# Queries and keys in parts: from float32 transposes to FR matmuls with a unit matrix, in a kernel of four transformer layers on one core

## The reference

```python
x = x + L0_xattn(ln(x), ctx)          # 16 heads of 8, cross attention
x = x + L0_ffn(ln(x))                 # norm, 8 experts of 512, gelu
x = x + L1_xattn(ln(x), ctx)          # 32 heads of 4, padding and key masks
x = x + L1_ffn(ln(x))                 # top 2 of 8 experts, with a capacity
x = x + L2_xattn(ln(x), ctx)          # 16 heads of 8, scores + slope * (i - j)
x = x + L2_ffn(ln(x))                 # int8 matmul with scales
x = x + L3_xattn(ln(x), ctx, itok)    # a decoder of 4 layers, see below
x = x + L3_ffn(ln(x))                 # top 1 of 8 experts
```

```python
q, k, v = split(rmsnorm(x) @ Wqkv.T + bqkv)
q, k = rope(q), rope(k)
x = x + softmax(q @ k.T * scale + causal) @ v @ Wo.T + bo
x = x + cross_attention(rmsnorm(x), ctx, lookback by itok)
x = x + silu(h @ Wg.T) * (h @ Wu.T) @ Wd.T      # h = rmsnorm(x)
```

## Time and profile before

| what | value |
|---|---|
| median of three timed runs | 2184.98 us (2182.89 to 2188.85) |
| profiled execution | 2199.41 us |
| its span, from first to last instruction | 2197.7 us |
| mean granted clock of PE | 0.906 |
| PE busy | 1863.2 us |
| DVE busy | 1451.6 us |
| ACT busy | 1065.8 us |
| POOL busy | 665.8 us |

### The profile page before, as it was taken

One profiled execution on the slowest core, in us unless ns is written; L12 is line 12 of the kernel. 1 busy time (PEld: TensorE's weight loads), 2 busy tenths in 40 slices (PEclk: granted clock), 3 DMA queues, 4 the chain that ended last, 5 costly groups with the idle time before them and its releaser, 6 DMA issues.

```text
span 2197.7 us, 34230 instructions
## 1 busy us (share of the span) xinstructions
PE 1863.2 (85%) x12747; PEld 1123.4 (51%) x12747; DVE 1451.6 (66%) x3531; ACT 1065.8 (48%) x1517; POOL 665.8 (30%) x903
## 2 busy tenths in 40 slices
PE   5977998575687888899989898999989989989977
PEld 4546665364453444565544464544455544456543
DVE  8645766553676767865576884567785466786468
ACT  3642665221443455564366556356656346656410
POOL 3111100512614444310454320345330244431030
PEclk9978999577787799999899999989999989999879
DMA  6441333121000000131000033000024000013100
GB/s 220 111 122 73 97 94 113 52 72 51 24 1 13 1 1 1 42 100 51 15 1 1 3 90 83 23 1 1 1 55 111 3 15 1 1 28 97 45 0 20
DMA packets 80745, 100.88 MB, mean 46 GB/s; under 512 B 31462, under 2 KB 46190, under 8 KB 79940
## 3 DMA queue, kind: packets, MB, share of 16 engines
q1 hardware_dynamic: 78532, 94.50, 15.1%
q0 software_dynamic: 2048, 4.20, 0.7%
HBM read 52.43 MB, written 12.38 MB: 29 GB/s over the span
## 4 chain that ended last, share of the span: by engine, by line
PE 41%; DVE 14%; ACT 6%; issue 5%; POOL 1%; SPq 1%; DMA 1%; DVEq 0%; POOLq 0%; ACTq 0%
PE wide L806 29%; PE acc L806 11%; DVE maxima L1732 6%; ACT prob L1974 2%; DVE hid L1235 1%; DMA masked_q<-q_g 1%; DVE x L1793 1%; DVE hid L1402 1%; DVE qkv L1700 1%; POOL rstd L2036 1%; DVE hn L1323 1%; ACT prob L1897 1%; SPq L730 1%; ACT hn L1862 1%; DVE hn L1325 1%
## 5 line engine op out<-in xcount | busy, mean ns | idle before, releaser
L1732 DVE TENSOR_REDUCE maxima<-wide 128x2 f32<-128x512 f32 (+3 forms) x512 | 406.7, 819 | 163.3 <-PE wide L806 160.4
L1974 ACT ACTIVATE prob<-wide 128x768 f32<-128x768 f32 (+1 forms) x384 | 332.9, 881 | 159.6 <-PE wide L806 158.7
L1897 ACT ACTIVATE prob<-wide 77x1024 f32<-77x1024 f32 x256 | 257.9, 1017 | 106.6 <-PE wide L806 105.8
L806 PE MATMUL wide<-q_g 32*128 32x256 f32 (+3 forms) x2048 | 275.1, 408 | 34.3 <-ACT prob L1974 16.1
L2198 POOL TENSOR_SCALAR_AFFINE_SELECT prob<-prob 128x256 f32<-128x256 f32 (+1 forms) x384 | 186.9, 490 | 359.1 <-ACT prob L1974 353.4
L1411 DVE TENSOR_REDUCE maxima<-wide 128x8 f32<-128x616 f32 x256 | 202.8, 795 | 112.8 <-PE wide L806 108.9
L2036 POOL TENSOR_TENSOR rstd<-moments,cst 128x4 f32<-128x4 f32 x88 | 89.8, 1020 | 543.9 <-DVE moments L1299 284.7
L806 PEld LDWEIGHTS wide<-q_g 32*128 32x128 f32 x2048 | 144.6, 197 | 214.2 <-issue 99.1
L1818 ACT ACTIVATE q_g<-wide 128x1024 fp32r<-128x1024 f32 x128 | 131.1, 1024 | 193.0 <-PE wide L806 193.0
L1818 ACT ACTIVATE q_g<-acc 128x512 fp32r<-128x512 f32 x192 | 114.4, 596 | 169.7 <-PE acc L806 165.8
L806 PE MATMUL wide<-kx,q_g 128*128 128x312 f32 x512 | 178.5, 414 | 7.7 <-DVE maxima L1411 4.8
(11 more groups left out here) (237 smaller groups left out, 3062.5 us busy)
## 6 DMA issues: line engine op xcount, KB each, us to landing
masked_q<-q_g SPq DMA_DIRECT2D x448, 64.0 KB
masked_q<-mask_l SPq DMA_DIRECT2D x84, 308.0 KB
masked_k<-kx SPq DMA_DIRECT2D x224, 19.5 KB, 2.3
A<-in_w SPq DMA_DIRECT2D x2, 2048.0 KB, 13.6
unit_w<-in_unit_w SPq DMA_DIRECT2D x8, 448.0 KB, 3.7
ffn_w<-in_ffn_w SPq DMA_DIRECT2D x4, 768.0 KB, 4.5
slots_in<-qkv SPq DMA_DIRECT2D x1, 2560.0 KB, 13.9
prob<-slots_in SPq DMA_DIRECT2D x8, 320.0 KB, 3.1
```

The costliest lines, as they stand in the source:

```text
L806: return e.matmul(out, lhsT, rhs, start=start, stop=stop, is_transpose=turn)
L1732: e.tensor_reduce(top[:, t, h], v[:, :, at0:at0 + P * t + P], AX.X, ALU.max, negate=True).then_inc(*made("max", *([("free", tile)] if t == ...
L1897: e.activation(p[0:SC, :], s[0:SC, :], ACT.Exp, bias=0.0, scale=1.0).then_inc(*made("exp", pb, ("free", tile)))
L1974: e.activation(pv, sv, ACT.Exp, bias=0.0, scale=8 ** -0.5).then_inc(*made("exp", pb, ("free", tile)))
```

## The change

The parts are written as FR. Two FR tensors `hid_parts0` and `hid_parts1` lie over the two buffers of `hid`, and `k_tok` becomes an FR tensor over the same place in A. The high part is no longer masked out but rounded: `top_part` is a copy from float32 to FR, for queries, keys and maxima (the keys of cross attentions keep `high_part`). A second unit matrix `ident_r` in FR is made at the start. `turn_queries` is a plain FR matmul with it instead of a transpose in float32. Since a matmul lets every column of the tile enter the sums, columns that no part fills have to be numbers: in units 1 and 2, with heads of 4, POOL clears these too. Memsets go through a float32 view. `clear` has seven steps in place of nine: it clears the columns from MROW on of `k_tok` and the rest of the buffer.

```diff
-CLEARS = 9
+CLEARS = 7
...
-        k_tok = A[:, 0:2048].rearrange("p (t h r) -> p t h r", t=NI, h=16)
+        k_tok = nc.alloc_sbuf_tensor_at("k_tok", [P, 2048], FR, offset=a_at)[:, :].rearrange(
+            "p (t h r) -> p t h r", t=NI, h=16)
...
+        hid_at = [-(-nc.sbuf_base // 32) * 32 + 4 * NI * S * n for n in range(2)]
         hid = bufs("hid", 2, lambda n: sb(f"hid{n}", [P, 4, S]))
+        hid_parts = [nc.alloc_sbuf_tensor_at(f"hid_parts{n}", [P, NI, S], FR, offset=at) for n, at in enumerate(hid_at)]
...
+        ident_r = sb("ident_r", [P, P], FR)
...
-            return hid[T.slot("hid", key)][:, :, :].rearrange("p t (h r) -> p t h r", h=16)
+            return hid_parts[T.slot("hid", key)][:, :, :].rearrange("p t (h r) -> p t h r", h=16)
...
-                    i_mm = mm(out[:, P * i:P * i + P], qt[:, i, h:h + HG, :].rearrange("p h r -> p (h r)"), ident,
-                              turn=True)
+                    i_mm = mm(out[:, P * i:P * i + P], qt[:, i, h:h + HG, :].rearrange("p h r -> p (h r)"), ident_r[:, :])
...
+            def top_part(out, src):
+                return e.tensor_copy(out, src)
...
+            e.tensor_copy(ident_r[:, :], ident).then_inc(*made("begin"))
...
-                high_part(high, src).then_inc(*made("q", ("q_top", n, b)))
+                top_part(high, src).then_inc(*made("q", ("q_top", n, b)))
...
-                high_part(v[:, :, :, MROW], top).then_inc(*made("max_in"))
+                top_part(v[:, :, :, MROW], top).then_inc(*made("max_in"))
...
-                high_part(qt[:, :, :, 0:PART], src).then_inc(*made("cut", ("sq_top", l, b)))
+                top_part(qt[:, :, :, 0:PART], src).then_inc(*made("cut", ("sq_top", l, b)))
...
-                high_part(k_tok[:, :, :, 0:PART], src).then_inc(*made("cut", ("sk_top", l, b)))
+                top_part(k_tok[:, :, :, 0:PART], src).then_inc(*made("cut", ("sk_top", l, b)))
...
-                e.memset(qt[:, :, :, MROW:HR], 0.0).then_inc(*made("q"))
+                e.memset(qt[:, :, :, MROW:HR].bitcast(F32), 0.0).then_inc(*made("q"))
+                if dh < PART:
+                    parts = qt[:, :, :, 0:MROW].rearrange("p t h (y r) -> p (t h) y r", r=PART)
+                    e.memset(parts[:, :, :, dh:PART].bitcast(F32), 0.0).then_inc(*made("q"))
...
+                if k == 0:
+                    e.memset(k_tok[:, :, :, MROW:HR].bitcast(F32), 0.0).then_inc(*made("clear"))
+                    return
                 if k < CLEARS - 1:
-                    e.memset(A[:, 640 * k:640 * k + 640], 0.0).then_inc(*made("clear"))
+                    e.memset(A[:, 640 * k + 1408:min(640 * k + 2048, 5120)], 0.0).then_inc(*made("clear"))
```

More of the change, by code:

```diff
@@ L475, in bufs @@
             return [make(i) for i in range(n)]
+        a_at = -(-nc.sbuf_base // 32) * 32
         A = sb("A", [P, 8192])
@@ L2066, in q_cut @@
                         e.wait_ge(*w)
-                    e.memset(qt[:, :, :, KROW:KROW + 1], 1.0).then_inc(*made("q"))
+                    e.memset(qt[:, :, :, KROW:KROW + 1].bitcast(F32), 1.0).then_inc(*made("q"))
                     e.tensor_copy(qt[:, :, :, QROW], const("position").unsqueeze(2).broadcast_to([P, NI, 16])).then_inc(
@@ L2129, in clear @@
                     e.wait_ge(*w)
-                e.memset(k_tok[:, :, :, MROW:MROW + 2], 1.0).then_inc(*made("clear"))
+                e.memset(k_tok[:, :, :, MROW:MROW + 2].bitcast(F32), 1.0).then_inc(*made("clear"))
                 for buf in v_self:
@@ L2176, in cut_q @@
                     e.wait_ge(*w)
-                e.memset(qt[:, :, :, MROW:HR], 0.0).then_inc(*made("cut"))
+                e.memset(qt[:, :, :, MROW:HR].bitcast(F32), 0.0).then_inc(*made("cut"))
                 for w in need(own(), ("sq_top", l, b)):
```

## The result

The changed kernel takes 2249.9 us (median of 4 runs, 2245.69 to 2259.68), the kernel before 2186.91 us in the same comparison: the ratio is 1.0289, with a 95% interval of 1.0256 to 1.0322. The change costs 63 us. The forecast was 2325 us, +140: the sign and the cause hold, the size is less than half.

What follows compares the result with a forecast made beforehand. TensorE, including its clock, was taken as the bound. From the profiled 2199.4 us, +4 for turns and casts, +136 for the falling clock and −14.4 to the timed median gave 2325 us, range 2180 to 2430.

Steps and rivals of the forecast that it cites:

- The pace: TensorE's 1792 turns: FR goes by the weight load, 107 ns a turn against 110 in float32; taken as no change.
- a burst's ends: 448 bursts of four turns: first load 58 ns longer, last stream 51 ns shorter, 7 ns a burst, +3 us.
- The casts: DVE rounding to FR instead of masking: wide casts +0.6 us, 16-column casts 0, FR unit matrix +0.5 us.
- The clock: TensorE's clock: FR turns stream 59 ns instead of 110, so self-attention stretches fall from 2.4 to 1.2 GHz; +136 us.
- The price: Cost of time at half clock: 0.33 us a microsecond, so full-clock work T takes 1.49 T at half.
- twins: The same steps in different layers at different clocks: 10.10 us at 1.00 against 12.20 at 0.72, and 9.70 against 12.10.
- the four stretches: Trace stretches taken as the self attentions: 159.6 + 3 × 144.7 = 594 us, of which 554 at full clock.
- How much falls: Self attentions: half of the 554 us at full clock falls to half clock, +136 us; cross attentions nothing.
- The clock that stays: Rival 1: TensorE's clock is unchanged by the FR turns; 2189 us, chance 0.11.
- Turns that hide their loads: Rival 2: weight loads hide under the turn before, a turn costs 59 ns instead of 110; 2148 us, chance 0.06.
- The clock that rises without transposes: Rival 3: the clock ignores transpose mode, so matmuls in its place lift it; −68 us, 2121 us, chance 0.05.
- The dear casts: Rival 4: 16-column casts take 460 ns, all on the path, clock unchanged; +33 us, 2222 us, chance 0.04.

Runs made afterwards that it cites:

- lengthened streams: Changed kernel with three of four turns streaming twice: 2198.9 us, 1.0049; with turns streaming up to thrice: 2246.7 us, 1.0255.
- streams from added matmuls: Changed kernel plus two unused bf16 matmuls ahead of each self-attention burst into acc: 2229.4 us, 1.0164.
- the kernels without the mask: Kernel before and changed kernel, each without the 768 bf16 causal mask matmuls of the maxima: 2211.7 us, 1.0117, and 2304.7 us, 1.0581.

## Why the prediction was right and wrong

- **The pace, right.** 112 ns a turn, as 110 before. For a burst's ends I had 7 ns, the first load's 58 less 51 at the last stream; over all bursts at full clock it was 12 to 20 ns, at most 9 us of PE time.
- **The casts, right.** They cost what the masks cost. With the turns undone all the rest of the change, the memsets too, is at 1.0014.
- **The clock, right in kind.** It fell with the turns' shorter streams, and the time with it; float32 turns, lengthened streams and streams from added matmuls each brought both back in the changed kernel, wholly or in part.
- **The price, about right.** 0.33 us a microsecond at half clock was forecast from twins; the four stretches lost 33 us (626.3 − 593.7) for 101 us more, 0.32, and 0.30 in the kernels without the mask. Over the whole kernel, by the medians and the runs' clocks, it is 63 / 237 = 0.27.
- **How much falls, wrong.** This is the step "Between none of it and all of it (554 × 0.49 = +271 us) no row decides; I take half, +136 us, and nothing for the cross attentions, where less is changed per microsecond." In the four stretches it was +33 us, for 101 us more at half clock. Half of 554 us would have been 277 us of work, which take 277 × 1.49 = 413 us at half clock: a quarter of that fell. In place of a share of all full-clock time, the clock fell in single steps: the earlier trace rows's step of 9.70 us stayed at 1.00, the one behind it fell to 0.61. The kernels without the mask agree with a reserve that a half ignores.
- **Where it falls, misread.** The four stretches were taken for the self attentions, with "768 in 594 us, 1.29 a microsecond". They leave out most of the first batch entry and hold 176 of the 256 key turns; of the 1792 turns that change, the trace before has 551 in them, 0.93 a microsecond against 0.77 in the rest. So the prediction had nothing for a part of the self attentions: with it they lost 39.8 us for 150 us more at half clock. The remaining 57 us at half clock came with 47.3 − 39.8 = 7.5 us; the kernel with FR in the cross attentions alone lost 14 us by the medians, where I had taken 0.
- **The rivals.** The clock that stays: no, 0.862. Turns that hide their loads: no, 112 ns. The clock that rises without transposes: no, it fell; with the transposes put back it stood at 0.909 by the runs. Here the Trainium skill, "TensorE: Matmul & The Clock Gate", Part 4 (PE-mode transpose), by which the transpose mode doesn't count as busy for the gate, differs from the measurement on these float32 tiles, and the measurement decides. The dear casts: no, 279 ns.

What stays open is which of the stretches falls in a given execution. The same steps of different layers fell or held in one trace, and no run here tells what decides it. Open too is how much of the added matmuls' time lies on the path.

## What to carry to other kernels

Where TensorE's granted clock changes over a kernel, the work that its array streams is part of what the kernel lives on: an edit that shortens it at the same pace can cost time though it saves none, so compare the granted clock stage by stage before and after. To size such a loss, don't take a share of all full-clock time: ask for each stretch what else runs there, and test the reserve by leaving other work out. Before a density is worked out from a stretch, count in the trace what the stretch holds. And read the clocks of all runs: one profiled execution can be among the slowest or the fastest of its kernel.

## What the runs showed that was not expected

- Fewer matmuls, slower kernel: without 768 mask matmuls the kernel before goes from 1 to 1.0117, the runs' clock from 0.913 to 0.867. In the four stretches 139 us more at half clock are about 44 us at 0.32, and the stretches grew by 18: the removed matmuls gave back some 26 us by this estimate.
- Executions of one and the same kernel differ by the clock: in one comparison the kernel before took 2172.61 us at 0.921 and 2200.48 us at 0.904. These are 28 us for 79 us at half clock, 0.35: the same price again, without any change to the kernel.
- Matmuls without a use, 39 us of them, leave the time of the kernel before where it was, while its clock rises (0.913 to 0.919 by the runs); in the changed kernel the same ones save 1.2%.
